# VectorE's slot in another order, the turned norms on ScalarE, the product with the reciprocals on GpSimd

## The reference

```python
def _ln(x, w):                        # and its kin: then scaled and shifted by the condition
    mu = jnp.mean(x, axis=-1, keepdims=True)
    var = jnp.mean(jnp.square(x - mu), axis=-1, keepdims=True)
    return (x - mu) * jax.lax.rsqrt(var + EPS) * w
x_norm = _ln(x, norm1_w) * (1 + sc_msa) + sh_msa
s = jnp.einsum('bqhd,bkhd->bhqk', q, k) * scale
a = jax.nn.softmax(jnp.where(mask, s, min), axis=-1)
x = x + g_msa * (jnp.einsum('bhqk,bkhd->bqhd', a, v) @ attn_out_W)
```

## Time and profile before

| | us |
|---|---|
| median of 3 runs | 1201.91 |
| lowest, highest | 1200.75, 1204.64 |
| the profiled execution | 1201.14 |
| its span in the trace | 1199.0 |

### The profile page before, as it was taken

One profiled execution on the slowest core, in us unless ns is written; L12 is line 12 of the kernel. 1 busy time (PEld: TensorE's weight loads), 2 busy tenths in 40 slices (PEclk: granted clock), 3 DMA queues, 4 the chain that ended last, 5 costly groups with the idle time before them and its releaser, 6 DMA issues.

```text
span 1199.0 us, 28596 instructions
## 1 busy us (share of the span) xinstructions
PE 1068.0 (89%) x11711; PEld 674.1 (56%) x11711; DVE 821.1 (68%) x2035; ACT 571.5 (48%) x801; POOL 598.0 (50%) x602
## 2 busy tenths in 40 slices
PE   7899999999888997989999688899888999999898
PEld 4445545555554774656666445555555556655476
DVE  6677777778774433756677668788887887787521
ACT  1133334465556434443444236465555556665563
POOL 5565665566754331111114468576565645566421
PEclk8899999999999997998999769899999999998999
DMA  4300000000001102000000000000000000000001
GB/s 171 125 2 2 19 11 11 19 11 19 16 14 29 36 27 83 12 6 6 6 6 12 11 12 2 1 2 2 2 1 1 2 2 2 2 2 2 1 27 44
DMA packets 9280, 22.88 MB, mean 19 GB/s; under 512 B 1392, under 2 KB 1648, under 8 KB 8768
## 3 DMA queue, kind: packets, MB, share of 16 engines
q1 hardware_dynamic: 9152, 21.07, 5.3%
HBM read 18.90 MB, written 2.15 MB: 18 GB/s over the span
## 4 chain that ended last, share of the span: by engine, by line
PE 66%; DVE 20%; issue 7%; ACT 3%; POOL 3%; DMA 0%; DVEq 0%; SPq 0%; POOLq 0%; ACTq 0%
PE weighed L631 10%; DVE negmax L1104 9%; PE row_scores L573 6%; PE scores L777 5%; PE scores L604 5%; PE weighed L654 5%; PE scores L530 4%; PE quads L511 3%; PE quads L537 3%; PE quads L522 3%; PE row_scores L777 3%; DVE bn L978 2%; PE scores L616 2%; PE row_scores L788 2%; PE scores L644 2%
## 5 line engine op out<-in xcount | busy, mean ns | idle before, releaser
L1104 DVE TENSOR_REDUCE negmax<-row_scores 128x8 f32<-128x616 f32 (+1 forms) x312 | 298.6, 957 | 83.7 <-PE row_scores L573 52.4
L1508 ACT ACTIVATE p<-scores 128x1024 f32<-128x1024 f32 (+1 forms) x256 | 247.6, 1018 | 218.7 <-PE scores L616 218.7
L1665 POOL TENSOR_TENSOR kblk_r<-work,pack_const 128x308 fp32r<-128x308 f32 (+1 forms) x160 | 134.2, 839 | 240.7 <-PE row_scores L573 216.4
L604 PE MATMUL scores<-qblk,work 32*77 32x512 f32 (+1 forms) x1280 | 205.8, 626 | 13.9 <-ACT p L1508 6.8
L573 PE MATMUL row_scores<-kblk_r,qr 32*128 32x308 f32 (+1 forms) x624 | 141.9, 444 | 54.3 <-DVE negmax L1104 51.6
L631 PE MATMUL weighed<-p,v 77*32 77x128 f32 (+1 forms) x5120 | 176.1, 279 | 2.7 <-DVE nat L1120 2.5
L1655 POOL TENSOR_TENSOR qblk<-work,pack_const 128x512 f32<-128x512 f32 x160 | 168.7, 1054 | 14.6 <-PE scores L604 13.6
L573 PEld LDWEIGHTS row_scores<-kblk_r,qr 32*128 32x128 f32 x624 | 63.8, 189 | 176.0 <-issue 101.9
L631 PEld LDWEIGHTS weighed<-p,v 77*32 77x32 f32 (+1 forms) x5120 | 132.1, 111 | 45.7 <-DVE nat L1120 22.0
L616 PE MATMUL scores<-nblk,select 32*77 32x512 f32 (+1 forms) x640 | 154.9, 808 | 0.0
L1508 ACT ACTIVATE p<-scores,neg_kb 77x1024 f32<-77x1024 f32 x64 | 67.6, 1105 | 52.3 <-PE scores L616 52.3
(11 more groups left out here) (287 smaller groups left out, 1841.9 us busy)
## 6 DMA issues: line engine op xcount, KB each, us to landing
shared<-gates_hbm SPq DMA_DIRECT2D x24, 256.0 KB, 3.2
shared<-in_ctx_tok SPq DMA_DIRECT2D x16, 154.0 KB
pack_w_l<-in_w_l SPq DMA_DIRECT2D x1, 2058.5 KB, 10.0
x<-in_x_tok SPq DMA_DIRECT2D x8, 256.0 KB, 6.2
out_x<-x SPq DMA_DIRECT2D x8, 256.0 KB, 2.0
layers_w<-in_w_l SPq DMA_DIRECT2D x1, 1289.0 KB, 9.1
ctxT<-in_ctxT SPq DMA_DIRECT2D x1, 1232.0 KB, 8.8
layers_w<-in_w_l SPq DMA_DIRECT2D x1, 640.0 KB, 6.4
```

The costliest lines, as they stand in the source:

```text
L604: mm = e.matmul(scores[0:nk, g, :], k_of[q % 3][at, s * nk:(s + 1) * nk], qblk[n % 2][at, :], start=layer.mask != "qk", stop=False, skip_g ...
L1104: e.tensor_reduce(negmax[q % 2][:, 2 * h:2 * h + 2, 0, s * NJ:(s + 1) * NJ], row_banks(n, h)[:, :, 0:NJ * nk].rearrange("p g (j k) -> p g ...
L1508: e.activation(p[n % 2][0:nk, 8 * h:8 * h + 8, :], scores[0:nk, 2 * h:2 * h + 2, :].rearrange("p g (j q) -> p (g j) q", j=NJ), ACT.Exp, bi ...
L1665: e.tensor_tensor(kblk_r[n % 2][:, 0:NJ * nk].rearrange("p (j k) -> p j k", j=NJ), k_of[q % 3][:, s * nk:(s + 1) * nk].unsqueeze(1).to_bro ...
```

## The change

1. VectorE's slot is written in another order. Both row maxima come first, always. The rotations and the spread maximum follow. Then `turn_blocks` and `invert` of job **t-1** (they were of t-2) and `turn_back` of job **t-2** (was t-3), then statistics, `take_x`, `residual`, `take_q`. The exception for masked slots is gone.
2. `normalise` moves from VectorE to the end of GpSimd's slot, for job t-1. It reads `nat` and `rden` and writes `attn`, as before.
3. `scale_normed` on VectorE and `shift_normed` on GpSimd are gone, and with them `hat` and `ln_scaled`. In their place ScalarE's `take_normed` does scale and shift at once, four activations a norm (one a sequence), from PSUM to the target. It stands behind the slot's exponentials and `round_q`, and TensorE's waits for `ln_scaled` are now waits for `ln_done`.

In `routed`, ScalarE's one call for slots -14 to -7 of phase 1 is split into four and these are spread between the hidden layers' activations. TensorE's instructions and their order are the same.

```diff
@@ tensor_program, in scores_read(t) and quads_read(t) alike
                     if t in norm_at and norm_at[t].family:
-                        w.wait_ge(ln_scaled, norm_at[t].index + 1)
+                        w.wait_ge(ln_done, norm_at[t].index + 1)
                     if cl == 2 and qi - 2 in quads and qi >= hi:
                         w.wait_ge(wo_read, qi - 1)
                     if cl == 2 and qi + 1 in quads:
...
@@ vector_program: removed
 
-            def scale_normed(it):
-                scale, _, ready, value = affine(it)
-                w.wait_ge(ready, value)
-                w.wait_ge(ln_turned, it.index + 1)
-                w.wait_ge(ln_done, it.index)
-                e.tensor_tensor(by_seq(hat[:, 0:it.cols]), by_seq(turned_bank(it)[:, 0:it.cols]),
-                                scale.unsqueeze(2).to_broadcast([128, QUAD, it.n]), ALU.mult).then_inc(ln_scaled, 1)
-
             def take_x(q):
...
@@ vector_program, attention(): one slot
                 for t in range(4 * lo + first, end):
                     qi, cl = divmod(t, QUAD)
-                    masked = t in jobs and layer_of(qi).mask == "qk"
-                    if t + 5 in jobs and not masked:
-                        row_max(t + 5, 1)
-                    if t - 2 in jobs:
-                        turn_blocks(t - 2)
-                    if t - 3 in jobs:
-                        turn_back(t - 3)
-                    if t - 2 in jobs:
-                        invert(t - 2)
-                    if t + 5 in jobs and masked:
+                    if t + 5 in jobs:
                         row_max(t + 5, 1)
                     if t + 6 in jobs:
                         row_max(t + 6, 0)
-                    if cl == 3 and qi + 1 in quads and not masked:
-                        spread_max(qi + 1)
-                    if t - 2 in jobs:
-                        normalise(t - 2)
                     if cl == 0 and qi + 2 in quads and layer_of(qi + 2).rope:
                         rotate(qi + 2, 1)
+                    if cl == 3 and qi + 3 in quads and layer_of(qi + 3).rope:
+                        rotate(qi + 3, 0)
+                    if cl == 3 and qi + 1 in quads:
+                        spread_max(qi + 1)
+                    if t - 1 in jobs:
+                        turn_blocks(t - 1)
+                    if t - 2 in jobs:
+                        turn_back(t - 2)
+                    if t - 1 in jobs:
+                        invert(t - 1)
+                    for it in STATS_AT.get((phase == 1, t), ()):
+                        take_stats(it)
                     if cl == 1 and qi + 3 in quads and layer_of(qi + 3).name == "l3c":
                         take_x(qi + 3)
                     if cl == 2 and qi - 2 in quads:
                         residual(qi - 2)
-                    if cl == 3 and qi + 3 in quads:
-                        if layer_of(qi + 3).rope:
-                            rotate(qi + 3, 0)
-                        elif not q_by_act(qi + 3):
-                            take_q(qi + 3)
-                    if t in norm_at:
-                        scale_normed(norm_at[t])
-                    if cl == 3 and qi + 1 in quads and masked:
-                        spread_max(qi + 1)
-                    for it in STATS_AT.get((phase == 1, t), ()):
-                        take_stats(it)
+                    if cl == 3 and qi + 3 in quads and not layer_of(qi + 3).rope and not q_by_act(qi + 3):
...
@@ scalar_program: new
+            def take_normed(it):
+
+                scale, shift, ready, value = affine(it)
+                w.wait_ge(ready, value)
+                w.wait_ge(ln_turned, it.index + 1)
+                if not it.kind in ("l0m", "l3f"):
+                    w.wait_ge(proj_v, it.q - 2)
+                    w.wait_ge(proj_q, it.q - 2)
+                    w.wait_ge(proj_k, it.q - 2)
+                for s in range(QUAD):
+                    at = slice(s * it.n, (s + 1) * it.n)
+                    done = e.activation(norm_target(it)[:, at], turned_bank(it)[:, at], ACT.Identity, bias=shift[:, s:s + 1],
+                                        scale=scale[:, s:s + 1])
+                done.then_inc(ln_done, 1)
+
             def take_q(q):
                 w.wait_ge(proj_q, q + 1)
                 w.wait_ge(qblk_done, 4 * (q - 3) + 4)
...
@@ scalar_program, attention(): one slot
                         take_v(qi + 1)
+                    if cl == 1 and qi + 2 in quads:
+                        round_q(qi + 2)
+                    if t in norm_at:
+                        take_normed(norm_at[t])
                     for it in roots:
                         if not it.family:
                             root(it)
-                    if cl == 1 and qi + 2 in quads:
-                        round_q(qi + 2)
                     if cl == 3 and qi + 3 in quads and q_by_act(qi + 3):
                         take_q(qi + 3)
                     if first_layer_at(t, hi) is not None:
...
@@ gpsimd: pool_program
 
-            def shift_normed(it):
-                _, shift, ready, value = affine(it)
-                w.wait_ge(ready, value)
-                w.wait_ge(ln_scaled, it.index + 1)
-                if it.kind in ("l2k", "l2", "l0", "l0c", "l3s"):
-                    w.wait_ge(proj_v, it.q - 2)
-                    w.wait_ge(proj_q, it.q - 2)
-                    w.wait_ge(proj_k, it.q - 2)
-                e.tensor_tensor(by_seq(norm_target(it)), by_seq(hat[:, 0:it.cols]),
-                                shift.unsqueeze(2).to_broadcast([128, QUAD, it.n]), ALU.add).then_inc(ln_done, 1)
+            def normalise(n):
+                w.wait_ge(rden_done, n + 1)
+                w.wait_ge(attnT_done, n - 1)
+                e.tensor_tensor(attn[n % 2][:, :].rearrange("p (k d) -> p k d", d=HD),
+                                nat[n % 2][:, :, :].rearrange("p i (k c) -> p (i k) c", c=16)[:, :, 0:HD],
+                                rden[n % 2][:, :].unsqueeze(2).to_broadcast([128, NH, HD]), ALU.mult).then_inc(attn_done, 1)
 
             def add_rows(c, row, done):
                 xs = x[:, c * QUAD:(c + 1) * QUAD, :]
@@ -1718,8 +1712,6 @@
                         add_rotated(qi + 2, 1)
                     if t + 7 in jobs:
                         spread_k(t + 7)
-                    if t - 1 in norm_at:
-                        shift_normed(norm_at[t - 1])
                     for it in XHAT_AT.get((phase == 1, t), ()):
                         normalise_x(it)
                         if it.kind == "l3f":
@@ -1735,6 +1727,8 @@
                         add_rows(qi % NB, layer.name + "_ob", x_biased)
                     if cl == 3 and qi - 2 in quads and layer_of(qi - 2).gated:
                         add_gated(qi - 2)
+                    if t - 1 in jobs:
+                        normalise(t - 1)
                     if phase == 0 and second_layer_at(t, hi) is not None:
                         add_perceptron(second_layer_at(t, hi))
                     if phase == 0 and t == 4 * hi + 11:
```

## The result

The changed kernel takes **1229.91 us** (median of 4 runs, 1226.19 to 1230.66), the kernel before 1203.15 (4 runs, 1200.75 to 1204.64). The ratio is **1.022, with a 95% interval of 1.019 to 1.025**: 2.2% slower, where 1190.0 was forecast, in a range that ended at 1204. The profiled execution has a span of 1228.9 us, against 1199.0.

What follows compares the result with a forecast made beforehand. TensorE, busy 1068.0 of 1199.0 us, was taken as the bound, idling for VectorE's row maximum. Terms -16.4 - 9.7 + 3.0 + 8.1 + 7.4 - 4.0 = -11.6 us gave 1190, likely 1184 to 1197, outer range 1176 to 1204.

Steps and rivals of the forecast that it cites:

- the 14 slots: Quads 8 to 11 and 18 to 27: new order starts VectorE's maximum about 1.17 us earlier each, 16.4 us gained.
- the three small operations: VectorE's transpose, back-transpose and reciprocal after the half-0 maximum in l3s: 0.67 us, ending near 883.4.
- at most 0.5: TensorE's waits for `negmax` in quads 8 to 11 and 18 to 27 would be at most 0.5 us.
- The masked slots: In l0 VectorE's transpose waits for weighing: 1.07 us lost in each of six quads, 0.85 in two, 8.1.
- take_q in quads 5 to 7: take_q now stands behind three transposes: 0.6 us lost in each of three l0 quads, 1.8 together.
- the 1.0 predicted for the rotations: In l0's cl = 0 the rotations move up by one product: 0.17 x 6 = 1.0 us gained.
- the masked slots decide: Rival, chance 0.14 for slower: l0's transpose wait plus clock dips costs 2.9 us a quad, 23 us, giving 1209.
- The clock: TensorE's clock dips behind long waits in the attention: fewer waits, fewer dips, 4.0 us gained, between -5 and 12.
- The dips vanish: Rival, chance 0.20: all eight attention dips go with the long waits, l0 stays at full clock: 1182 us.
- The norms: Four ScalarE activations replace a norm's scale and shift: 0.36 us each, 1.46 us together at most.
- The 3.0 us put on the phase ends as loss: At phase ends TensorE waits for ScalarE's norms behind the exponentials: 3.0 us lost, between 0 and 5.
- the 3.0 as gain: GpSimd's shift leaves the chain of waits at the turn of the phases and the start: 3.0 us gained.

Runs made afterwards that it cites:

- e1: The changed kernel with three attnT buffers instead of two, nothing else: 1188.48 us, ratio 0.9856 to the kernel before.
- e6: The kernel before with only the statistics put ahead of the residual add in slots that aren't masked: 1171.45 us, ratio 0.9764.
- e11: The changed kernel with third attnT buffer, masked slots' statistics and residual ahead of the transpose, and norms back on VectorE and GpSimd (ScalarE split kept): 1185.13 us.
- e5: The kernel before with only the product with the reciprocals moved to the end of GpSimd's slot, still job t-2: 1191.3 us, ratio 0.9923.
- e4: The kernel before with only the turned norms moved to ScalarE, including the split of ScalarE's run-up to the second phase: 1192.64 us, ratio 0.9892.
- e10: The kernel before with norms on ScalarE, product on GpSimd, unmasked statistics ahead of the residual, masked half-1 maximum ahead of the transposes: 1165.91 us, ratio 0.9694.
- e7: The changed kernel, two buffers kept, with only masked slots reordered (statistics and gated residual ahead of job t-1's transpose): 1214.19 us, ratio 1.0151.

## Why the prediction was wrong

**The step that failed** is the working of the 14 slots, in its sentence "the three small operations take 169.47 - 168.80 = 0.67 us, so they end near 883.4". It took the duration of the three from a place where none of them waits, and moved them, without asking for each what it waits for in the new slot. The wait stood in `turn_back`; the order of its slot was what had satisfied it for nothing. The term, -16.4, became a loss of 5.2: the waits at that place rose by 0.37 us each in the 14 slots, to 1.65 in l0c, 1.70 in l2 and 2.03 in l3s, and also in quads 28 to 37, where I had put nothing. e1 and e6 show the term itself to be right, with waits of 0.00, 0.16 and 0.48 to 0.60 where "at most 0.5" was predicted.

**The masked slots.** 8.1 us were predicted. Summed over the eight quads, TensorE's waits at cl = 3 went from 4.81 to 12.85 us, 8.0 more. But l0 became 14.5 us longer: four dips of the clock, 1.6 each, and 2.5 us of take_q in quads 5 to 7 (1.8 predicted) came on top, and some 2.4 us went elsewhere in these slots, of which I can place the 1.0 predicted for the rotations at most. The rival "the masked slots decide" had both, and argued against itself with the absence of dips before, when no wait was that long.

**The clock** is the term whose sign was wrong: -4.0 predicted, about +10 in the changed kernel (14 dips for 8). That dips go with waits over 1.2 us held in one direction: each of the 14 begins at the end of a wait of 1.58 to 2.07 us or up to 2 us behind it. It is no rule in the other: in l0 the wait of 1.76 in quad 3 has no dip behind it, and e6 keeps five waits over 1.2 without one. "The dips vanish" (chance 0.20) was half right for the kernel that I had drawn: in e1 the dips of l0c and of quads 16 to 29 are gone, but l0 has four.

**The norms.** Four activations took 1.49 to 1.53 us together, against 1.46. Their mean by the page is 460 ns, but they overlap; it is the group's length that counts, and it is what the row scaling gave. The estimate of 1.6 us by the Trainium skill (ScalarE: Activation LUTs, section Rules for kernel authors) is above it by 0.1. The 3.0 us put on the phase ends as loss and the 3.0 as gain were both too small: quads 38, 39 and the end lost 4.2, quads 14, 15 and the middle won 7.2. That gain I had put down to the norms; by e11 most of it belongs to the split of ScalarE's run-up or to the new order, to which I had given no price there.

**GpSimd.** The product costs 405 ns, where 0.45 was taken and 0.40 was the lower bound, and what it makes late for TensorE is small: e5 has 3.5 us of matmuls waiting for `kblk_r`, against 2.2 before. VectorE's busy time ended at 738.0 instead of 711: a product's 283 ns overlap its neighbours, and e5 took off 56.7 us for 160, 0.354 each, not 0.45, which is 15 of the 27 us; e4 took off 37.5 for the scales, near the 38.6 predicted. The other 11 stay open. Before, some products on VectorE took up to 1121 ns, and in e4, where they stay there, up to 1172; on GpSimd the longest is 411. The Trainium skill (SBUF — State Buffer, section SBUF: two separate sides) says that a VectorE instruction with two SBUF inputs and one of GpSimd exclude each other. The trace agrees: the product of 1121 ns, at 747.81 in quad 18, ends 0.22 us behind a GpSimd instruction that ran beside it. But e10 shows that with the norms off VectorE those long ones cost nothing that the time shows.

**Added up**, by the table: start +5.3 (scatter), l0 +14.5, l0c +1.7, turn of the phases -7.2, quads 16 to 29 +7.3, quads 30 to 37 +4.1, end +4.2, in all 29.9, the difference of the spans. With the third buffer the same kernel is at 1188.5, near the 1190.0 forecast, but that is luck and not the forecast's sum: masked dips cost more, the unmasked ones and the turn of the phases gave more. Two readings were off without weight in the sum: the 5.1 us of l0c's four waits are L568's and no part of the 51.6 of L573, and the clock of 0.63 is the mean over 4 us of the earlier trace rows, not the lower level, which is 0.50 in the window of 2 us within.

What stays open: why the start takes 67 or 72 us in programs with the same start; what the split of ScalarE's run-up is worth by itself; and which share of the 4 us at the end is the norms' and which the order's (e4, e11 and e7 give 2.1, 3.0 and 5.3, with a dip more or less in each).

## What to carry to other kernels

When an operation moves to an earlier slot, write down every wait that it carries, buffers that it fills included, and find where in the new slot each is met; a wait that cost nothing in the trace of before has no row there, and an in-order engine lays it on all that stands behind it. Change one place in the order at a time: one moved statement (e6) gave 28 us, and the whole change, which contains it, lost 27. Where TensorE's clock falls behind long waits, a wait that goes is worth more than its length: here 19.1 us of waits went for 28 of time (e6), and 26.7 for 41 (e1). An edit that carries a second one with it, as e4 does the split, can't say which of the two gave the time.

## What the runs showed of the hardware

- The granted clock falls behind single waits of TensorE: one of 1.76 us with 0.48 us of work in 2 us before (l0), and in l0 of the kernel before not behind waits of up to 0.73. Between them it is no matter of the wait alone: e6 keeps five of 1.25 to 1.36 in quads 17 to 19, 35 and 36 and has no dip there, the kernel before has the same five and a dip behind two of them, and one more behind a wait of 0.81 in quad 37.
- Four activations of 128 columns that follow each other take 1.50 us and of 77 columns 1.33, though each is listed with 460 and 414 ns: in a row they start every 0.35 and 0.30 us.
- GpSimd's product reading pieces of 8 columns costs 396 to 411 ns for 128 columns. Its rows of 308 and 512 columns (702 and 1041 ns) give some 400 for 128 in one piece, by a straight line, which is an estimate; by it the pieces cost nothing.
